# A head's scores masked, scaled and reduced in one VectorE instruction, its row sum on ScalarE, in the attention of a small vision transformer

## The reference

```python
h = tok_ref(x, ...)                                  # patches @ W + b, class token, positions
h = h + attn_ref(layernorm(h), Wq, Wk, Wv, Wo)
h = h + ffn_ref(layernorm(h), ...)                   # 2 shared + top 4 of 16 routed experts, gelu

# attn_ref: 8 query heads, 4 key/value heads of 128
q = q * cos + rotate_half(q) * sin                   # k likewise
attn = einsum('bhtd,bhsd->bhts', q, k) / sqrt(128)
attn = where(causal, -inf, attn)
attn = softmax(attn, axis=-1)
out = einsum('bhts,bhsd->bhtd', attn, v)             # then @ Wo
```

## Time and profile before

| | |
|---|---|
| three runs | 158.98, 159.10, 159.22 us, median 159.1 us |
| profiled execution | 159.16 us, of which the span of the trace is 157.2 us |
| busy, share of the span | PE 150.4 us (96%), PEld 140.9 (90%), DVE 125.3 (80%), ACT 95.5 (61%), POOL 63.6 (40%) |
| granted TensorE clock | 0.997 of full speed over the span |
| chain that ended last | PE 83%, DVE 12%, issue 2%, ACT 1% |

### The profile page before, as it was taken

How to read it: one execution, slowest core, us unless ns; L and a number is a source line. 1 busy time by engine, 2 the same in 40 slices (tenths; PEclk the granted TensorE clock), 3 DMA queues, 4 the chain that set the end, 5 groups by cost and what they waited for, 6 DMA issues and landing times.

```text
span 157.2 us, 3252 instructions
## 1 busy us (share of the span) xinstructions
PE 150.4 (96%) x1101; PEld 140.9 (90%) x1101; DVE 125.3 (80%) x336; ACT 95.5 (61%) x230; POOL 63.6 (40%) x62
## 2 busy tenths in 40 slices
PE   6999979999999999999999999999999999999990
PEld 2888669888999997999989999999999999999990
DVE  0035987879899999999894756889996897969993
ACT  0305878899667885976184299687446646575220
POOL 0005997556458573293910000139243542630300
PEclk9999999999999999999999999999999999999998
DMA  5999900000000007992000000000000000000004
GB/s 153 324 378 363 383 12 4 2 2 4 0 0 0 4 0 255 425 422 105 2 0 4 0 2 0 0 0 4 0 6 0 0 0 4 0 0 0 0 4 154
DMA packets 5745, 11.86 MB, mean 75 GB/s; under 512 B 914, under 2 KB 3682, under 8 KB 5602
## 3 DMA queue, kind: packets, MB, share of 16 engines
q1 hardware_dynamic: 4434, 9.91, 17.2%
q10 hardware_dynamic: 1296, 1.75, 3.1%
HBM read 11.05 MB, written 0.61 MB: 74 GB/s over the span
## 4 chain that ended last, share of the span: by engine, by line
PE 83%; DVE 12%; issue 2%; ACT 1%; DVEq 0%
PE bank L1070 62%; PE bank L1085 6%; PE bank L1162 4%; PE bank L1189 4%; DVE h L830 2%; PE bank L1078 2%; PE bank L1174 2%; DVE qk L718 1%; PE bank L1158 1%; PE bank L1213 1%; DVE stats L679 1%; DVE hn L701 1%; DVE qk L725 1%; DVE ssum L753 1%; PE bank L1114 1%
## 5 line engine op out<-in xcount | busy, mean ns | idle before, releaser
L393 POOL TENSOR_TENSOR exp_lo<-ffn_sb,exp_hi 128x512 fp32r<-128x512 f32 x18 | 24.3, 1355 | 49.3 <-ACT exp_hi L510 48.3
L830 DVE SCALAR_TENSOR_TENSOR h<-bank,gate,h 128x256 f32<-128x256 f32 (+1 forms) x80 | 32.5, 473 | 1.1 <-PE bank L1070 1.0
L1070 PE MATMUL bank<-exp_hi,act_hi 128*128 128x256 f32 (+1 forms) x90 | 25.4, 282 | 0.0
L1070 PE MATMUL bank<-exp_lo,act_hi 128*128 128x256 f32 (+1 forms) x90 | 25.3, 281 | 0.0
L1070 PE MATMUL bank<-exp_hi,act_lo 128*128 128x256 f32 (+1 forms) x90 | 25.2, 280 | 0.0
L377 POOL TENSOR_TENSOR swapped<-swapped,sin_sb 128x296 f32<-128x296 f32 x24 | 20.0, 837 | 12.5 <-ACT swapped L482 12.2
L810 DVE TENSOR_TENSOR act_lo<-act,act_hi 128x256 fp32r<-128x256 f32 (+1 forms) x36 | 18.4, 527 | 5.6 <-ACT act_hi L522 4.9
L519 ACT ACTIVATE act<-bank 128x256 f32<-128x256 f32 (+1 forms) x36 | 15.3, 424 | 11.8 <-PE bank L1070 11.4
L1070 PE MATMUL bank<-hnT_hi,exp_hi 128*128 128x256 f32 (+1 forms) x72 | 21.9, 304 | 0.0
L1070 PE MATMUL bank<-hnT_hi,exp_lo 128*128 128x256 f32 (+1 forms) x72 | 21.5, 299 | 0.0
L1070 PE MATMUL bank<-hnT_lo,exp_hi 128*128 128x256 f32 (+1 forms) x72 | 21.5, 298 | 0.0
(11 more groups left out here) (96 smaller groups left out, 369.9 us busy)
## 6 DMA issues: line engine op xcount, KB each, us to landing
ffn_sb<-w_ffn SPq DMA_DIRECT2D x6, 768.0 KB, 7.9
wqkv_sb<-w_qkv SPq DMA_DIRECT2D x4, 512.0 KB, 8.6
wo_sb<-w_o SPq DMA_DIRECT2D x1, 1024.0 KB, 11.0
x_sb<-xT ACTq DMA_DIRECT2D x3, 192.0 KB, 4.9
x_sb<-xT SPq DMA_DIRECT2D x3, 192.0 KB, 4.8
out<-h SPq DMA_DIRECT2D x2, 256.0 KB, 2.2
wp_sb<-wpT SPq DMA_DIRECT2D x3, 128.0 KB, 4.4
wp_sb<-wpT ACTq DMA_DIRECT2D x3, 128.0 KB, 5.1
```

Source lines behind the costliest of these rows:

```text
L393: nc.gpsimd.tensor_tensor(exp_lo[:, e % SPLIT_RING, :], ffn_sb[:, e, :], exp_hi[:, e % SPLIT_RING, :].bitcast(F32), ALU.subtract).then_inc ...
L830: last = nc.vector.scalar_tensor_tensor(h[r, i, :], y, gate[r, i, one], h[r, i, :], ALU.mult, ALU.add)
L1070: last = nc.tensor.matmul(ps, a, b, start=(n == 0 and m == 0), stop=(n == len(pairs) - 1 and m == 2 and not more))
```

## The change

The mask is no longer a matrix product. For each head one VectorE instruction takes the scores from the bank, scales them with -1/sqrt(128), adds the mask (now in the sense that makes forbidden places large), writes the result to SBUF and its row minimum, which is the negative scaled maximum, to `slow`. ScalarE then does exp(-x + `slow`) for each head, with the row minimum as its bias, and writes the row sum to `ssum`. The sums on VectorE are gone, and so are the two casts that made the mask and the identity in bf16.

```diff
@@ exps
-                nc.scalar.activation(quad(probs, g, c), quad(probs, g, c), ACT.Exp, scale=SCALE).then_inc(sc_exp, 1)
+                for j in range(QUAD):
+                    hd = QUAD * c + j
+                    scores_of = probs[0:GN[g], g % 2, hd, 0:GN[g]]
+                    last = nc.scalar.activation(scores_of, scores_of, ACT.Exp, bias=slow[0:GN[g], g, hd:hd + 1], scale=-1.0,
+                                                accum_out=ssum[0:GN[g], g, hd:hd + 1])
+                last.then_inc(sc_exp, 1)
@@ less_max
-                nc.vector.tensor_reduce(smax[0:GN[g], g, QUAD * c:QUAD * c + QUAD], quad_bank(2 + c, g),
-                                        AX_X, ALU.max).then_inc(sc_max, 1)
-                dve.wait_ge(sc_max, 2 * g + c + 1)
...
-                nc.vector.tensor_tensor(quad(probs, g, c), quad_bank(2 + c, g), per_head(smax, g, c),
-                                        ALU.subtract).then_inc(sc_less, 1)
+                for j in range(QUAD):
+                    hd = QUAD * c + j
+                    last = nc.vector.tensor_tensor_reduce(
+                        probs[0:GN[g], g % 2, hd, 0:GN[g]], bank[2 + c][0:GN[g], j * GN[g]:(j + 1) * GN[g]],
+                        mask_f[0:GN[g], 0:GN[g]], -SCALE, -MASKED, ALU.add, ALU.min, slow[0:GN[g], g, hd:hd + 1])
+                last.then_inc(sc_less, 1)
@@ inv_sum
-                nc.vector.tensor_reduce(ssum[0:GN[g], g, QUAD * c:QUAD * c + QUAD], quad(probs, g, c),
-                                        AX_X, ALU.add).then_inc(sc_sum, 1)
-                dve.wait_ge(sc_sum, 2 * g + c + 1)
@@ scores
-                nc.tensor.matmul(quad_bank(2 + c, g), ident_b[0:GN[g], 0:GN[g]],
-                                 mask_b[0:GN[g], :, 0:GN[g]], start=True, stop=False, skip_group_check=True)
                 for j in range(QUAD):
...
-                                            start=False, stop=(j == QUAD - 1), skip_group_check=True)
+                                            start=True, stop=True)
@@ the lists of calls, on VectorE at the front
             norm_stats(2)
+            norm_stats(3)
             norm_apply(1)
             norm_apply(2)
-            turned_low(0)
-            norm_stats(3)
+            for n in range(0, 3):
+                turned_low(n)
             norm_stats(4)
-            turned_low(1)
-            turned_low(2)
```

More of the change, by code:

```diff
@@ L1031, in _ @@
             add_expert(10, 1)
-            for n in range(23, 27):
+            for n in range(22, 26):
                 act_low(n)
@@ L1266, in _ @@
             turn_norm(2)
-            for n in range(0, 3):
+            for n in range(0, 4):
                 project(n)
@@ L1340, in _ @@
             turn_norm(8)
-            for n in range(0, 4):
+            route(1)
+            for n in range(0, 3):
                 up(n)
             turn_norm(9)
-            for n in range(1, 4):
-                route(n)
+            up(3)
+            route(2)
+            route(3)
             up(4)
@@ L1372, in _ @@
             down(6, 2)
-            for n in range(14, 19):
+            down(7, 0)
+            for n in range(17, 21):
                 up(n)
-            down(7, 0)
             down(7, 1)
@@ L1387, in _ @@
             down(10, 1)
-            for n in range(23, 27):
+            down(10, 2)
+            for n in range(25, 28):
                 up(n)
-            down(10, 2)
             down(11, 0)
@@ L1406, in _ @@
             down(14, 2)
+            for n in range(32, 35):
+                up(n)
             down(15, 0)
             down(15, 1)
-            up(34)
             up(35)
```

328 lines of the change are left out of this document (158 added, 170 removed).

## The result

| | median | lowest to highest | runs |
|---|---|---|---|
| before | 159.01 us | 158.61 to 159.36 | 20 |
| after | 159.62 us | 159.10 to 160.45 | 20 |

What follows compares the result with a forecast made beforehand. The bound was taken as TensorE's instruction stream plus under 2 us of waits. Masks -2.1, front -0.2, wait at 61.4 -0.45 and new waits +0.5 made -2.25: 159.16 to 156.9 us, range 156.1 to 160.2.

Steps and rivals of the forecast that it cites:

- This is saved in full as long as its inputs come 2.1 us earlier too: TensorE, attention stage: removing 12 mask products saves 2.1 us; bounds nothing and 2.1.
- New waits +0.5 us: TensorE would lose 0.5 us waiting for ScalarE's copy of turned quad (1,1), wanted at 58.4, ending at about 59.
- because it arrives no earlier than they do: TensorE at group 3's scores: the 0.43 us wait at 61.41 for the last rotated heads goes, counted as -0.45.
- ScalarE's quad, 1.42 us forecast: Exponentials of four heads of one group, 111 rows: 1.42 us, between 0.80 and 2.23, bias at 57 ns each.
- VectorE's quad, 1.37 us forecast: Four masked-score and row-minimum pairs on VectorE: 1.37 us, between 1.06 and 1.68, no effect on the end.
- Front -0.2: Before the first projection: tile 4's statistics after three splits, so the split of tile 2 ends 0.2 us earlier.
- The experts at nothing: Experts' stage: same instructions at the same pace, 66 us unchanged, last two splits falling where ScalarE is free.
- The slope of 8.5 us for 1 us of quad, and the break-even of 1.68: ScalarE's exponentials from 41 us: 1 us more a quad costs 8.5 us; no gain left at 1.68 us.
- all hidden: Rival: at or under 1.3 us a quad on ScalarE the new waits go, 156.4 us; chance 0.15.
- the gain is eaten nearly whole: Rival: ScalarE's quad takes 1.55 to 1.7 us, +1.7 us of waits, 158.6 us; chance 0.15.
- ScalarE becomes the bound: Rival: swaps and copies behind exponentials (0,1) to (3,1), from 1.68 us a quad; 160.1 us at 1.8; chance 0.20.
- The signs of a wrong forecast: Exponentials starting 420 ns or more apart, ScalarE never idle from 41 to 72 us, TensorE waiting before projections 20 to 23, groups 1 to 3.

Runs made afterwards that it cites:

- e4: The kernel before with its 12 mask products taken out and nothing else changed: 158.46 us, ratio 0.9973.
- e15: e8 with the 12 mask products and their two casts put back beside VectorE's own mask: 160.11 us, ratio 1.0052 to before.
- e10: e8 with the row sums given back to VectorE, exponentials still head by head with bias: 159.38 us, ratio 1.0020 to before.
- e1: After's kernel with the front's lists of calls put back to the order of before: 159.30 us, ratio 1.0022 to before.
- e6: After's kernel with the order of before in the routed experts: 159.39 us, ratio 1.0029 to before.
- e14: e8 with one wide exponential a quad, without bias, maximum or row sum (sums a constant): 157.90 us, ratio 0.9917 to before.
- e8: After's kernel with before's order in front and experts, and turned quad (1,1) behind projection piece 23: 158.71 us, ratio 0.9982 to before.
- e11: e8 with one wide exponential a quad on ScalarE; masked scores, subtraction and row sums on VectorE: 168.15 us, ratio 1.0559 to before.
- e18: e2 with quad (2,0)'s exponentials, reciprocal and product moved behind the swaps of pieces 20 and 21: 165.32 us, ratio 1.0378 to before.
- e13: The instructions of e11 in the order of the kernel before: 164.98 us, ratio 1.0365 to before.
- e2: After's instructions in the order of the kernel before on all four engines: 164.57 us, ratio 1.0358 to before.

## Why the prediction was wrong

- **"This is saved in full as long as its inputs come 2.1 us earlier too":** this is the term that failed. They don't come earlier. The products' worth was 0.4 us in the old order (e4), where VectorE had been busy for 24.33 of 25.40 us, and 1.1 in the mended new one (e15), where VectorE has 3.4 us free and ScalarE 1.1. The condition stood in the sentence, and so did the bound of nothing. The sum went by the upper bound without following the condition through the engines that feed TensorE, first ScalarE, which the change itself filled.
- **New waits +0.5 us:** 3.0 us in the trace, four places with 2.5. The copy of the turned quad (1,1) was there: forecast to end at about 59 (the terms named for it add up to 58.5), it ended at 60.20, because ScalarE also had gaps of over 0.2 us at 44.5 and 57.7 us where it waited for TensorE. It does not act alone: the last rotated head is ready at 61.22 only. I had written that the wait for it would be gone, "because it arrives no earlier than they do"; it is still there, 2.68 us from the end of piece 23 as against 2.81. I also missed what is ahead, pieces 20 and 22 waiting for the cosines of 18 and 20. I had counted ScalarE's instructions up to one place and didn't follow the pair of banks through which every second piece is let in.
- **ScalarE's quad, 1.42 us forecast:** right in size, 1.49 and 1.37. That its work would just fit was right too. By the rows the bias is 83 ns (380 against an interpolated 297; 381 in e10, which has the bias and no row sum), not 57, and the row sum 0.09 us start to start. The size came out nearly right with one part too low and another left to the overlap.
- **VectorE's quad, 1.37 us forecast:** 0.78. It has more room than I thought, and that did not help.
- **"Front -0.2":** +0.4 (e1). The split of tile 2 does start as soon as ScalarE's copy ends (19.85 us), but ScalarE's two small steps on tile 4 now stand behind a swap and a copy, and the turning of tiles 3 and 4 takes 0.65 us longer.
- **The experts at nothing:** +0.25 (e6; 0.37 in the traces), a step I had set at zero without cover by any row.
- **The slope of 8.5 us for 1 us of quad, and the break-even of 1.68:** the kernel was slower at 1.49, below the break-even. For shorter quads I had let 0.5 us come back ("all hidden"); 1.0 us less a quad gives 1.0 us (e14 against e8). Upwards it wasn't measured.
- **The rivals:** "the gain is eaten nearly whole" and "ScalarE becomes the bound" were tied to a quad over 1.55 us. The outcome was theirs, the size of the quad wasn't. "All hidden", and the estimate of 1.21 us beside it, counted no instruction for the row sum and fell. The signs of a wrong forecast were half met: ScalarE nearly without idle time and TensorE waiting before projections 20 and 22 and in group 1, but with starts 0.37 us apart and not 0.42.

The ways in the traces show where the 2.1 us went. From the first projection piece to what follows piece 23, from there to scores (3,1), and from there to the last matmul, in us, one trace each:

| kernel | to the end of piece 23 | to scores (3,1) | to the last matmul | sum |
|---|---|---|---|---|
| before | 37.49 | 2.81 | 91.57 | 131.87 |
| of it mask products | 1.23 | 0 | 0.85 | 2.08 |
| e4 (before without them) | 36.71 | 3.14 | 91.24 | 131.09 |
| after | 38.23 | 2.68 | 91.79 | 132.70 |
| e8 (three pieces put back) | 37.61 | 2.68 | 91.42 | 131.71 |
| e14 (e8 with a wide exponential) | 37.06 | 2.68 | 90.93 | 130.67 |

In the measure of the ratios, e8 stands 0.3 us below before (its interval reaches no change). The three pieces of the new order cost 1.0 us (e8 against after) and ScalarE's exponentials 1.0 (e14 against e8), each give or take 0.5. What is left of the 2.1 us, 0.8, no run here brought back. The table places it: e14 needs 37.06 us to the end of piece 23, where before less its mask products would need 36.26, and it loses nothing in the stretch behind. So it lies in waits ahead of the end of piece 23. The largest that shows is in front of piece 22, 0.78 us from the turned quad to it where before has 0.32. Longer additions of the rotated heads (649 ns in e14, 458 before) may be behind them, which isn't shown.

## What to carry to other kernels

When work is taken off the engine that bounds a stage, look first at the engines next in line. VectorE had 1.1 us free of 25.4, and 2.1 us taken off TensorE gave 0.4; with more room on VectorE and ScalarE full they gave 1.1. A condition such as "as long as its inputs come earlier too" has to be worked out for each engine that feeds the path, or the term goes in at a lower value. In a kernel whose order is written out by hand, instructions and order are one thing: either alone in the other's company cost 5.6 us, so a change of durations has to be priced with its order, and a bad result of one without the other says little. A wait that is found can lie within another: ask, for each, what would release the engine next if it went. Once an engine is without a gap, a small step that another engine can take in an idle moment (0.6 us moved, 0.5 us gained) was worth more here than either reordering of swaps on the full one.

## What the runs showed of the hardware

A row sum on ScalarE is an instruction of its own, 192 ns long, of which 0.09 us shows in the distance of the starts. On VectorE the reader of the row minimum (82 ns) disappears: the pairs start 0.19 us apart, under the 268 ns of the first alone.

A VectorE sum of two SBUF tensors of 296 columns takes 0.46 us by itself. In after, the one beside GpSimd's product of a quad (0.93 us from 43.34) reads

```profile
43.58 1.01 DVE L724 TENSOR_TENSOR qk<-qk,swapped 128x296 f32<-128x296 f32 x1
```

and the mean over 15 is 555 ns in after, 721 in e11, 458 before. In e11 one takes 1.78 us from 45.67; GpSimd has two products one behind the other from 45.43 to 47.13, and the sum ends 0.3 us behind them, as if it had stood until they were through. The Trainium skill ("GPSIMD Engine Reference", section "Specifications") says that GpSimd's SBUF interfaces are shared with VectorE, with contention where a VectorE instruction has two SBUF inputs. The rows agree: the cosine's instruction, with one input from a bank, keeps its 0.46 us in after. The order decides which instructions meet: in e11 the 15 sums took 4 us more than before (15 x 0.26). How much of that TensorE waited for isn't shown.

TensorE's granted clock can fall from 2.4 to 1.2 GHz behind a wait in the middle of a kernel. It was 0.50 in e18 from 62 to 68 us, after TensorE had stood for 2.26 us, and low behind waits of 2.46 and 1.81 us in e11 and 2.17 us in e13; in the traces of before, after, e2 and e8 it stays at 1.00 through the attention stage. A wait of that kind costs more than its length: in e18 3.1 us on top.
